# Half steps for Gram, hidden, expert and cross products in a one-core layer, and a new sequence of its steps

## What is computed

```python
# cross attention: linear, no softmax
score = jnp.einsum('bhqd,bhkd->bhqk', Q, K) / dk
attn = jnp.where(mask, -jnp.inf, score)
ctx = jnp.einsum('bhqk,bhkd->bhqd', attn, V)
x = residual + _linear(ctx, wo_w, wo_b)          # then a layer norm
# causal self attention: softmax(q k^T * scale + bias) v, projected
# feed-forward part: rope attention, rms norm, shared network and experts
flat = _rmsnorm(src + sa, norm1_w)
shared = _swiglu(flat @ W_shared_in) @ W_shared_out
g_probs = jax.nn.softmax(flat @ Wg_gate + group_bias, -1)
g_idx = jnp.argmax(g_probs, axis=-1)
e_probs = jax.nn.softmax(jnp.where(in_group, e_logits, -jnp.inf), -1)
topv, topi = jax.lax.top_k(e_probs * g_prob, TOPK)
h = _swiglu(flat @ W1_shared)
for e in range(E):
    routed = routed + h @ W2_experts[e] * w[:, e:e + 1]
out = _rmsnorm(flat + shared + routed, norm2_w)
```

## Time and profile before

| | |
|---|---|
| median of 3 runs | 241.22 us (241.12 to 241.95) |
| span of the profiled execution | 239.0 us |
| PE busy | 228.0 us, 95% |
| DVE busy | 171.9 us, 72% |
| ACT busy | 121.4 us, 51% |
| POOL busy | 75.3 us, 32% |

### The profile page before, as it was taken

The page is one execution under the profiler, slowest core; times in us unless marked ns, Lnnn a source line. Parts: engine busy times, 40 slices in busy tenths (PEclk is TensorE's granted clock), DMA queues, the critical chain, the costliest instruction groups (busy, mean ns, idle before and its releaser), DMA issues.

```text
span 239.0 us, 5721 instructions
## 1 busy us (share of the span) xinstructions
PE 228.0 (95%) x2304; PEld 205.4 (86%) x2304; DVE 171.9 (72%) x370; ACT 121.4 (51%) x245; POOL 75.3 (32%) x89
## 2 busy tenths in 40 slices
PE   6989899999999999999999999999999999999991
PEld 6987797999999889978989999988878879998881
DVE  0757876966987879887966789586697764448353
ACT  3754575238571766386177977815451553550000
POOL 3011026222634020513549567745110020731011
PEclk9999999999999999999999999999999999999998
DMA  6899999828153452023304511100000000000001
GB/s 221 265 298 394 353 357 320 300 85 268 75 175 102 106 174 71 21 69 109 88 4 118 170 70 32 58 1 3 0 3 0 3 0 3 0 22 3 3 0 66
DMA packets 9434, 26.35 MB, mean 110 GB/s; under 512 B 1464, under 2 KB 2752, under 8 KB 9280
## 3 DMA queue, kind: packets, MB, share of 16 engines
q1 hardware_dynamic: 9120, 25.47, 32.4%
q10 hardware_dynamic: 288, 0.52, 0.6%
HBM read 25.46 MB, written 0.52 MB: 109 GB/s over the span
## 4 chain that ended last, share of the span: by engine, by line
PE 83%; DMA 7%; issue 3%; ACT 3%; DVE 2%; SPq 1%; POOLq 0%; POOL 0%; DVEq 0%
PE ps L704 77%; DMA raw<-in_ctx 7%; PE ps L707 5%; ACT ch L578 1%; DVE cl L1143 1%; ACT probT L511 1%; SPq L403 0%; DVE Z L1304 0%; SPq L358 0%; POOLq L363 0%; POOL rstd L463 0%; ACT z0T L511 0%; DVE X L1313 0%; DVE mb L1184 0%; DVE xHL L1273 0%
## 5 line engine op out<-in xcount | busy, mean ns | idle before, releaser
L704 PE MATMUL ps<-ch 128*128 128x130 f32 (+1 forms) x208 | 51.4, 264 | 1.5 <-DVE cl L1143 1.4
L704 PE MATMUL ps<-ch,cl 128*128 128x260 f32 (+1 forms) x208 | 51.1, 308 | 0.0
L704 PE MATMUL ps<-w,hT 128*128 128x512 f32 (+1 forms) x204 | 45.9, 382 | 0.0
L704 PEld LDWEIGHTS ps<-w,hT 128*128 128x128 f32 x204 | 36.4, 188 | 7.7 <-issue 0.7
L1143 DVE TENSOR_TENSOR cl<-raw,ch 128x1024 fp32r<-128x1024 f32 (+4 forms) x31 | 31.9, 1051 | 14.9 <-ACT ch L578 14.7
L704 PEld LDWEIGHTS ps<-ch 128*128 128x128 f32 (+1 forms) x208 | 39.5, 190 | 2.9 <-issue 1.4
L704 PEld LDWEIGHTS ps<-ch,cl 128*128 128x128 f32 (+1 forms) x208 | 39.2, 188 | 0.2
L463 POOL TENSOR_TENSOR rstd<-ve,half_exp 128x1 f32<-128x1 f32 (+1 forms) x22 | 13.8, 628 | 73.0 <-DVE ve L1022 72.9
L578 ACT ACTIVATE ch<-raw 128x1024 fp32r<-128x1024 f32 (+4 forms) x31 | 27.5, 916 | 12.9 <-DMA raw<-in_ctx 10.8
L704 PE MATMUL ps<-xHL,dense 128*128 128x256 f32 x192 | 24.3, 285 | 0.0
L704 PEld LDWEIGHTS ps<-xHL,dense 128*128 128x128 f32 x192 | 23.4, 192 | 0.2
(11 more groups left out here) (161 smaller groups left out, 417.7 us busy)
## 6 DMA issues: line engine op xcount, KB each, us to landing
raw<-in_ctx SPq DMA_DIRECT2D x22, 512.0 KB, 4.6
raw<-in_w SPq DMA_DIRECT2D x8, 512.0 KB, 3.8
stage<-in_dense SPq DMA_DIRECT2D x4, 512.0 KB, 5.9
w<-in_w SPq DMA_DIRECT2D x4, 256.0 KB, 6.9
w<-in_w SPq DMA_DIRECT2D x1, 1024.0 KB, 8.4
mask<-in_mask SPq DMA_DIRECT2D x1, 800.5 KB, 7.5
raw<-in_ctx SPq DMA_DIRECT2D x8, 65.0 KB
raw<-in_ctx ACTq DMA_DIRECT2D x2, 256.0 KB, 4.7
```

Source lines behind the costliest of these rows:

```text
L704: return pe.matmul(o, l, r, start=start, stop=stop, skip_group_check=not check)
```

## The change

Four kinds of PE steps become two steps each, with the same matmuls: `gram` is cut into `gram_rows` (row tiles 0 and 1, 8 matmuls) and `gram` (row tiles 2 and 3 and the tail), `hidden_product` into `hidden_half` and `hidden_product` (6 and 6), `experts_product` into `experts_half` and `experts_product` (6 and 6; the very last expert product 12 and 12), and `cross2_product` into `cross2_half` and `cross2_product` (2 and 2, with 4 more for odd batches). The waits stand on the first of the two, the signal on the second. The numbers of the squares, which were counted while the list was walked, are counted ahead, so that a root may stand ahead of its square in the list. All four lists are replaced by a new sequence.

```diff
@@ opening_steps (first_half_steps, second_half_steps, closing_steps likewise)
-        ("split", 0), ("split", 1), ("gram", 0), ("gram", 1), ("split", 2), ("gram", 2), ("split", 3), ("split", 4),
+        ("gram_rows", 0), ("gram", 0), ("split", 0), ("gram_rows", 1), ("gram", 1), ("gram_rows", 2), ("split", 1),
...
@@ split_products
-            def split_products(o, pairs):
+            def split_products(o, pairs, first=True, last=True):
                 todo = [(l[a], r[c]) for l, r in pairs for a, c in ((0, 0), (0, 1), (1, 0))]
                 for k, (l, r) in enumerate(todo):
-                    last = mm(o, l, r, k == 0, k == len(todo) - 1)
-                return last
+                    done = mm(o, l, r, first and k == 0, last and k == len(todo) - 1, first and last)
+                return done
@@ TensorE, gram
-                elif step == "gram":
+                elif step in ("gram_rows", "gram"):
                     b, c = divmod(i, CH_B)
                     banks = GRAM_B if b else CROSS_B
-                    if b > 1 and c == 0:
+                    if b > 1 and c == 0 and step == "gram_rows":
                         pe.wait_ge(sem("g"), b)
-                    for r in range(ROWS):
+                    for r in range(ROWS // 2) if step == "gram_rows" else range(ROWS // 2, ROWS):
...
-                    if c == CH_B - 1:
-                        last = gram_tile(banks, c, ROWS, TAIL, False, True)
-                    last.then_inc(sem("gram_chunk"), 1)
+                    if step == "gram":
+                        if c == CH_B - 1:
+                            last = gram_tile(banks, c, ROWS, TAIL, False, True)
+                        last.then_inc(sem("gram_chunk"), 1)
@@ TensorE, cross2
-                elif step == "cross2_product":
-                    pe.wait_ge(sem("gs"), i + 1)
-                    if i:
-                        pe.wait_ge(sem("ctxT"), i)
-                    else:
-                        pe.wait_ge(sem("wv_in"), 16)
+                elif step in ("cross2_half", "cross2_product"):
+                    ib = 0 if step == "cross2_half" else 1
+                    if ib == 0:
+                        pe.wait_ge(sem("gs"), i + 1)
+                        if i:
+                            pe.wait_ge(sem("ctxT"), i)
+                        else:
+                            pe.wait_ge(sem("wv_in"), 16)
...
@@ TensorE, hidden (the waits for xL, piece_low and taken stand on side 0 alone)
-                elif step == "hidden_product":
+                elif step in ("hidden_half", "hidden_product"):
...
+                    side = 0 if step == "hidden_half" else 1
...
-                    for side in range(2):
...
+                    if side == 1:
+                        last.then_inc(sem("products"), 1)
@@ TensorE, experts (the waits for h_low, piece_low and taken stand on the first half)
+                    if len(parts) > 1:
+                        split_products(o, hid).then_inc(sem("products"), 1)
+                    elif step == "experts_half":
+                        split_products(o, hid[:2], last=False)
+                    else:
+                        split_products(o, hid[2:], first=False).then_inc(sem("products"), 1)
@@ VectorE
-            square_of = {}
+            squares = [item for item in plan if item[0] in ("square", "last_square")]
+            square_of = {item: k + 1 for k, item in enumerate(squares)}
...
-                elif step in ("square", "last_square"):
-                    square_of[step, i] = len(square_of) + 1
```

More of the change, by code:

```diff
@@ L117, in second_half_steps @@
     return [
[L118 to L131, removed]
[3 rows of a table removed]
-        ("values1", 2), ("turn_x", 1), ("cross4", 7), ("piece", 8), ("score_product", (2, 0)), ("score", (2, 0)),
@@ L136, in second_half_steps @@
[L136 to L155, removed]
@@ L156, in second_half_steps @@
-        ("experts", (1, 2)), ("experts", (1, 3)),
+        ("norm1", 1), ("norm1_end", 1), ("split", 18), ("cross2", 4), ("split", 19), ("split", 20), ("gram", 17),
+        ("turn_z", (0, 1)), ("cross2_half", 4), ("cross2_product", 4), ("turn_z", (1, 0)), ("proj2_product", 0),
+        ("proj1_product", 1), ("evac", 5), ("rotate", 0), ("queries", 1), ("keys1", 1), ("values1", 1), ("roped", 0),
+        ("keys2", 0), ("keys_roped", 0), ("score_product", (1, 0)), ("values2", 0), ("score", (1, 0)), ("cross3", 4),
@@ new lines, in second_half_steps @@
+        ("exp", (1, 0)), ("gram_rows", 18), ("gram", 18), ("gram_rows", 19), ("shares", (1, 0)), ("gram", 19),
+        ("gram_rows", 20), ("cross1", 5), ("score", (0, 1)), ("score_product", (0, 1)), ("split", 21),
+        ("turn_p", (1, 0)), ("cross4", 4), ("gram", 20), ("piece", 2), ("exp", (0, 1)), ("shares", (0, 1)),
+        ("values", (1, 0)), ("piece", 3), ("evac", 6), ("cross2_half", 5), ("project", (1, 0)), ("norm2", 1),
+        ("cross2_product", 5), ("norm2_end", 1), ("split", 22), ("cross2", 5), ("split", 23), ("turn_p", (0, 1)),
@@ new lines, in second_half_steps @@
+        ("gram_rows", 21), ("turn_z", (1, 1)), ("values", (0, 1)), ("proj2_product", 1), ("project", (0, 1)),
+        ("rotate", 1), ("rms1", 0), ("cross3", 5), ("square", 0), ("roped", 1), ("keys2", 1), ("values2", 1),
+        ("keys_roped", 1), ("gram", 21), ("rms1_end", 0), ("cross1", 6), ("cross4", 5), ("turn_x", 0),
+        ("score_product", (1, 1)), ("gram_rows", 22), ("xo_product", 2), ("cross2_half", 6), ("piece", 4),
+        ("score", (1, 1)), ("exp", (1, 1)), ("gram", 22), ("gram_rows", 23), ("gram", 23), ("xo", 2), ("evac", 7),
[3 rows of a table added]
@@ new lines, in second_half_steps @@
+        ("rms1_end", 1), ("turn_z", (2, 0)), ("piece", 6), ("cross3", 7), ("turn_x", 1), ("piece", 7),
+        ("proj1_product", 2), ("cross4", 7), ("gates", 0), ("gate_groups", 0), ("keys1", 2), ("hidden_half", 0),
+        ("queries", 2), ("hidden_product", 0), ("xo", 3), ("xo_end", 3), ("norm1", 3), ("xo_product", 3),
+        ("piece", 8), ("piece", 9), ("hidden", 0), ("hidden_half", 1), ("hidden_product", 1), ("hidden_half", 2),
+        ("hidden_product", 2), ("hidden_half", 3), ("hidden_product", 3), ("values1", 2), ("hidden_half", 4),
@@ new lines, in second_half_steps @@
+        ("norm1_end", 3), ("hidden", 1), ("hidden", 2), ("turn_z", (3, 0)), ("score_product", (2, 0)), ("hidden", 3),
+        ("queries", 3), ("gate_experts", 0), ("exp", (2, 0)), ("proj1_product", 3), ("score", (2, 0)),
+        ("shares", (2, 0)), ("hidden_product", 4), ("hidden_half", 5), ("hidden_product", 5), ("hidden_half", 6),
+        ("hidden_product", 6), ("hidden_half", 7), ("keys1", 3), ("hidden", 4), ("hidden", 5), ("values1", 3),
+        ("hidden", 6), ("hidden_product", 7), ("shared_product", 0), ("hidden", 7), ("shared", 0), ("score", (3, 0)),
@@ L162, in closing_steps @@
     return [
[L163 to L167, removed]
```

122 lines of the change are left out of this document (75 added, 47 removed), and 6 rows, old and new, of the table USES.

## The result

The changed kernel takes 254.82 us (median of four runs, 254.02 to 255.53), against 241.20 for the kernel before: 1.0551 times as long, 95% interval 1.0518 to 1.0584. The forecast was 251.2, and the range ended at 254.5, 0.3 us under the median. The profiled run took 254.29 us with a span of 252.5, 13.5 longer than before.

The account below looks back on a forecast made before the run. PE's queue was taken as the bound, busy 223.8 of 228.2 us. Terms +1.8 - 1.6 + 2.1 + 2.4 + 3.3 + 2.0 = +10.0 gave span 249.0, median 251.2 us; range 244.5 to 254.5.

Parts of the forecast that it names:

- The halves: Products cut in two make PE change between kinds of matmul 117 times, before 95: 22 x 0.08 = +1.8 us.
- The opening: PE's waits in the opening: 1.7 us against 3.3, most filled, a new one at cross2_half 0; -1.6 us.
- 44 to 131 us: PE waits 3.8 us against 1.7, mainly at xo_product 1, turn_z (1,0) and turn_z (1,1): +2.1 us.
- Place A: score_product (2,0), about 144 us: POOL's subtractions of pieces 5 to 7 hold the ctxT add and `eg<-lg,gm`; +2.4 us.
- Place B: shared_product 0, about 156 us: second gate chain held by piece 9's and four `hT` subtractions; +3.3 us.
- Place C: turn_z (3,1), about 177 us: piece 12's subtraction behind norm2 3's root holds DVE's `Z<-X,mv,rstd`; +2.0 us.
- The end: The last product, the root and the store keep their sequence: 0.
- The clock: Rival: PE's clock falls at place B's wait, 2 to 3 us of matmuls take twice their time; 253 to 254.5, chance 0.07.
- the least certain term: Whether DVE's `Z<-X,mv,rstd` at turn_z (3,1) is held by piece 12's subtraction: 0.1 to 2.0 us, taken as 2.0.

Follow-up runs that it names:

- the short fills: Changed kernel with 7, 13 and 13 idle PE matmuls ahead of score_product (2,0), shared_product 0 and turn_z (3,1): 251.55 us, 1.0424 of before.
- POOL's own order: Changed kernel with another list for POOL alone, several weight piece subtractions moved, all work done: 246.30 us, 1.0207 of before.
- fills that only write: Changed kernel with POOL filling the left over part of all 13 weight pieces with zeros instead of subtracting: 241.94 us, 1.0016 of before.

## Why the prediction was right, and where it was off

The direction and the mechanism held: POOL's subtractions, put in rows, hold small DVE instructions, and PE waits at the three places named. Step by step, forecast and measured:

- **The halves**, +1.8: some 1.0, what is left of PE's 5.6 us of added busy time when the half clock's 4.6 are taken off.
- **The opening**, -1.6: -1.5 in PE's idle time.
- **44 to 131 us**, +2.1: +2.6.
- **Place A**, +2.4: 2.1. **Place B**, +3.3: 1.4. **Place C**, +2.0: 3.2. Together 7.7 forecast, 6.7 measured.
- **The end**, 0: the last matmul moved from 234.2 to 247.7, 13.5 as the span did.
- **The clock**, 0 in the sum, and a rival of chance 0.07 with 2 to 3: 4.6, of which 1.6 behind place A and 3.0 behind place C.

The measured terms add up to 13.4 of the 13.5 us between the two spans; the forecast had 10.0.

The step that failed is the clock. I left it out of the sum since earlier waits of up to 1.0 us had not brought it down, and named only the 3.3 of place B as a wait that might. In fact it fell behind the 1.75 of place A, where I had a wait of 2.0 on paper, and again behind place C. The trace of before had no wait between 1.0 us and the tail, where the clock did fall, so a forecast with three waits of 2 us and more should have carried the clock as likely. No row of before showed how long the half clock would last; the 2 to 3 us of the rival were short of the 3.4 and 6.9 measured. The 1.6 behind place A lengthened nothing, since PE lost them ahead of a wait (place B) that was shorter by as much. The net cost is the 3.0 behind place C, most of the 3.6 us by which the forecast was short; the short fills gave back 3.3.

The halves were put too high: 0.08 for each change between kinds of matmul came from one pair of rows (1.52 and 1.44), and the 1.0 that is left is nearer the 0.9 that the prediction gives when half of the changes cost nothing; no run isolates it. Place B was sized nearly right: with the clock whole ahead of it, PE waited 2.97 there, and the 1.36 of the changed kernel is what the 1.6 of half clock left of it. At C the sum left out piece 11, which holds the conversion in gate_best, an instruction whose form had not been seen held. With piece 12 moved away alone, PE still waited 1.26 there; with piece 11 and others moved as well, in POOL's own order, no wait is left. That the whole rest comes from piece 11 no run shows by itself. That the time came out no further from the forecast is in part luck: B, made shorter by the clock, and the halves offset what the clock and C added.

On the least certain term the measurement decides: `Z<-X,mv,rstd` was held whole, 2.35 us. The Trainium skill's "SBUF — State Buffer", section "Who interferes with whom", lets an instruction with one input in SBUF contend only in a mode that takes both ports, and names copy, cast and tensor_scalar as instructions that can enter it. The prediction used only the first half, and had the term possibly at zero by it. The Z instruction is a tensor_scalar; its hold, that of the conversion (2.10), and the hold by fills that only write (1.90) agree with what the section says of instructions inside that mode. That they ran in it no trace shows: unheld, the Z instruction took 0.41 us, hardly less than a tensor_tensor of that size (0.42). The same section of the Trainium skill has a second input contend with reads alone; the ctxT add beside such a fill (0.43) agrees.

What stays open is why the clock fell behind place A in the profiled run of the changed kernel and not in that with piece 12 moved, where the same wait of 1.75 us stood before it.

## What to carry to other kernels

Where VectorE and GpSimd share a long schedule, lay out their meetings before anything else: an instruction of 0.17 us stood for nearly 2 us here when GpSimd had just begun a long one, and a chain of small instructions (the gates) was held again at each link. Work that kept its time beside a GpSimd subtraction was a sum (`sm<-prob`, 1.22) and a subtraction that reads PSUM (`prob<-ps,mx`, 1.23 at 161.0 us, beside piece 10's), so such work is a better neighbour for long GpSimd instructions. Waits of the matrix engine of 1.75 and 3.2 us were followed by half clock that cost 1.6 and 3.0 more; fill such a wait or remove it, and expect that the next wait in line inherits what one removal gives back. Price a new order part by part: here the opening gained 1.1 us by itself, and was hidden under a loss made elsewhere.

## What the runs showed of the hardware beyond what I had expected

A GpSimd fill that reads nothing held a VectorE instruction with one SBUF tensor and two columns (1.90 us for 0.41), and not one with two tensors (0.43). A conversion of 16 numbers per partition (0.17 us unheld) was held for 2.10 us by a subtraction, and for 0.68 by a fill of 0.95 that had begun 0.30 earlier. PE's clock stood at half for 3.4 us behind a standstill of 1.75 us and for 6.9 us behind one of 3.2, both beginning about 0.5 us after PE had resumed; with idle matmuls in the same waits it stayed whole. By the same matmuls in both runs these 10.3 us cost 4.6. In another run the same standstill of 1.75 us was followed by whole clock.
